# Projecting the keys and values of all heads ahead of their use and keeping them in DRAM, with the attention unrolled in steps of half a head

## What is computed

```python
x = x + jnp.tanh(g_xattn[0]) * _L0_xattn_ref(_layernorm(x), ids, ctx, ctx, ctx)
x = x + jnp.tanh(g_ffn[0]) * _L0_ffn_ref(_layernorm(x), w_gate, w_up, w_down)

# attention: b = 4 sequences, sq = skv = 256, H = 16 heads of HD = 128
q = (inputs_q @ Wq).reshape(b, sq, H, HD) * (1.0 / np.sqrt(HD))
k = (inputs_kv @ Wk).reshape(b, skv, H, HD)
v = (inputs_kv @ Wv).reshape(b, skv, H, HD)
scores = jnp.einsum('bqhd,bkhd->bhqk', q, k)
attn = jax.nn.softmax(scores, axis=-1)
ctx = jnp.einsum('bhqk,bkhd->bqhd', attn, v).reshape(b, sq, H * HD)
return ctx @ Wo
```

## Time and profile before

| | before |
|---|---|
| three executions | 628.35, 634.35, 634.07 us, median 634.07 |
| profiled execution | 627.44 us, of it the span 625.5 us |
| mean granted TensorE clock | 0.963 |
| PE busy | 548.1 us (88%) |
| DVE busy | 433.7 us (69%) |
| ACT busy | 312.3 us (50%) |
| POOL busy | 279.2 us (45%) |

### The profile page before, as it was taken

How to read it: one execution, slowest core, us unless ns; L and a number is a source line. 1 busy time by engine, 2 the same in 40 slices (tenths; PEclk the granted TensorE clock), 3 DMA queues, 4 the chain that set the end, 5 groups by cost and what they waited for, 6 DMA issues and landing times.

```text
span 625.5 us, 9791 instructions
## 1 busy us (share of the span) xinstructions
PE 548.1 (88%) x3396; PEld 475.5 (76%) x3402; DVE 433.7 (69%) x850; ACT 312.3 (50%) x602; POOL 279.2 (45%) x278
## 2 busy tenths in 40 slices
PE   1989668986789999999999999999955948999995
PEld 1777457765678999999999999999853747777773
DVE  6768899898745555655565655555579494888884
ACT  2620124653455555565555556555523723676772
POOL 2499055781044535356443444633326540544440
PEclk9999789998989999999999999999997979999999
DMA  8601000000001111010010100000002007777731
GB/s 267 228 1 34 0 2 1 1 1 1 2 1 33 35 26 43 27 43 17 10 42 25 42 25 25 1 26 9 2 28 74 1 0 245 237 232 234 248 125 67
DMA packets 26646, 38.51 MB, mean 62 GB/s; under 512 B 3696, under 2 KB 18160, under 8 KB 26608
## 3 DMA queue, kind: packets, MB, share of 16 engines
q1 hardware_dynamic: 26608, 38.01, 19.0%
HBM read 36.82 MB, written 1.18 MB: 61 GB/s over the span
## 4 chain that ended last, share of the span: by engine, by line
PE 66%; DVE 18%; issue 7%; ACT 5%; POOL 2%; DMA 1%; SPq 0%; DVEq 0%; POOLq 0%; ACTq 0%
PE ps L1158 20%; PE ps L1160 19%; PE ps L1159 19%; PE ps L1199 4%; DVE xr L867 2%; PE ps L1266 2%; DMA cT_raw<-in_ctx_t 1%; PE ps L1250 1%; DVE ln_y L787 1%; DVE st L771 1%; DVE h L792 1%; DVE ln_t L785 1%; DVE qtok L890 1%; ACT q2T L691 1%; DVE a_sel L853 1%
## 5 line engine op out<-in xcount | busy, mean ns | idle before, releaser
L511 POOL TENSOR_TENSOR probs<-probs,rsum 128x512 f32<-128x512 f32 x64 | 66.7, 1042 | 151.1 <-DVE rsum L937 147.3
L672 ACT ACTIVATE probs<-ps,nmax 128x256 f32<-128x256 f32 x128 | 59.3, 472 | 38.7 <-DVE nmax L932 38.7
L912 DVE TENSOR_TENSOR pT_lo<-ps,pT_hi 128x512 fp32r<-128x512 f32 x64 | 43.6, 683 | 13.1 <-ACT pT_hi L663 13.0
L754 ACT ACTIVATE e_hi<-e_r 128x1024 fp32r<-128x1024 f32 x32 | 33.9, 1061 | 34.4 <-PE ps L1160 24.6
L932 DVE TENSOR_REDUCE nmax<-ps 128x2 f32<-128x512 f32 x64 | 42.6, 686 | 9.8 <-PE ps L1160 9.8
L1126 DVE SCALAR_TENSOR_TENSOR e_r<-ps,cw_row 128x1024 f32<-128x1024 f32 x32 | 39.2, 1224 | 14.0 <-PE ps L1160 14.0
L458 POOL TENSOR_TENSOR w_hi<-w_raw,zeros 128x256 fp32r<-128x256 f32 x32 | 20.1, 628 | 59.4 <-PE ps L1160 38.1
L663 ACT ACTIVATE pT_hi<-ps 128x512 fp32r<-128x512 f32 x64 | 37.9, 598 | 14.7 <-PE ps L1199 14.7
L1199 PE MATMUL ps<-cst,probs 128*128 128x128 f32 x256 | 38.7, 277 | 2.3 <-POOL probs L511 2.3
L1158 PE MATMUL ps<-wv_hi,cT_lo 128*128 128x256 f32 x128 | 37.9, 296 | 3.0 <-DVE kT_lo L907 3.0
L1136 DVE TENSOR_TENSOR e_lo<-ps,e_hi 128x1024 fp32r<-128x1024 f32 x32 | 38.9, 1215 | 1.9 <-ACT ps L755 1.9
(11 more groups left out here) (246 smaller groups left out, 1872.9 us busy)
## 6 DMA issues: line engine op xcount, KB each, us to landing
cw_row<-cw_scratch SPq DMA_DIRECT2D x32, 512.0 KB, 4.9
wqk_raw<-in_w_qk SPq DMA_DIRECT2D x16, 256.0 KB, 2.7
w_raw<-in_w_t SPq DMA_DIRECT2D x32, 128.0 KB, 4.6
wv_raw<-in_w_v SPq DMA_DIRECT2D x8, 256.0 KB, 3.2
wo_raw<-in_w_o SPq DMA_DIRECT2D x16, 128.0 KB, 2.0
xr<-in_x SPq DMA_DIRECT2D x2, 512.0 KB, 6.0
cT_raw<-in_ctx_t SPq DMA_DIRECT2D x1, 1024.0 KB, 7.6
wraw<-in_w_gate_t SPq DMA_DIRECT2D x1, 1024.0 KB, 7.9
```

Source lines behind the costliest of these rows:

```text
L511: nc.gpsimd.tensor_tensor(probs[:, b, :, :], probs[:, b, :, :], rsum[:, b, :].unsqueeze(2).to_broadcast([P, 2, S]), ALU.mult).then_inc(pro ...
L672: last = nc.scalar.activation(probs[:, b, t, :], ps[:, bank[u], t * S:(t + 1) * S], ACT.Exp, bias=nmax[:, b, t:t + 1], accum_out=esum[:, b ...
L754: nc.scalar.activation(e_hi[e % 2][:, :], e_r[e % 2][:, :], ACT.Square).then_inc(e_hi_done, 1)
L912: ins = V.tensor_tensor(pT_lo[:, half, :, :].rearrange("p c q -> p (c q)"), src, pT_hi[:, half, :, :].rearrange("p c q -> p (c q)").bitcas ...
```

## The change

Keys and values of all 16 heads are projected outside the attention's own steps. They are 64 "units" of six matmuls of 512 columns: a K unit is one head and half of the tokens, a V unit four heads and 128 tokens. `FILLS` says where TensorE makes them: 22 in the expert and BitNet stages (after expert tiles 1, 2 and 6, after gate tiles 0, 1 and 2, and so on) and 42 in the first 21 attention steps, one in the middle ("m") and one at the end ("e") of a step. ScalarE copies each from PSUM to `kv_out` (four buffers), SP stores it to `k_scratch` or `v_scratch` in DRAM, and loads `k_raw` and `v_raw` of a head two or three steps before its use; ScalarE then makes the high part of these, GpSimd the low part. VectorE no longer makes low parts of keys and values.

The weights come as 23 blocks of 128x1024 (512 KB), each for four heads and one of K, V, Q, O, through two buffers `blk_raw`; ScalarE makes the high part (`block_high`), GpSimd the low part (`block_low`). Key and value blocks are loaded twice where both halves need them. `STEP_OF_BLOCK` says in which of the attention's steps a block is loaded and split.

The attention is 32 unrolled steps. Step u has the scores of u (one head, tokens of half u // 16), the transposes of u - 1, the query of u + 2, the output of u - 1 and the `Wo` product of u - 2. The banks are fixed by kind instead of a ring. The first half of the tokens is added to `xr` at step 18, so two accumulating banks suffice. The Hadamard matrices come by a load of their own. `Y0_PAIR` and the pairs of the BitNet stage differ, since banks 0 and 1 hold units in between. The transposes Q of the first tokens stand in a pair of the expert layer.

```diff
-        STEP = ["S0", "S1", "Y0", "S2", "K0", "S3", "K1", "T0", "Y1", "T1", "V0", "T2",
-                "Q0", "Q1", "T3", "O0", "V1", "O1"]
...
+        Q_BANK, S_BANK, P_BANK, O_BANK, Y_BANK, N1_PAIR = [0, 1], [2, 3], [4, 5], 1, [6, 7], 6
+        Y0_PAIR = [6, 2, 4, 6, 2, 4, 6, 0]
...
+        STEP_OF_BLOCK = {0: 10, 1: 11, 2: 12, 3: 13, 4: 14, 5: 15, 6: 16, 7: 17, 9: 18, 11: 19, 13: 20, 15: 21, 17: 22}
...
+        FILLS = {"a11": 1, "y2": 1, "y6": 4, "g0": 2, "g1": 1, "f0": 6, "g2": 1, "f1": 2, "d5": 1, "n0": 1, "d6": 2}
+        FRONT_UNITS = sum(FILLS.values())
+        for k in range(FRONT_UNITS, NF):
+            FILLS["me"[(k - FRONT_UNITS) % 2] + str((k - FRONT_UNITS) // 2)] = 1
...
+            def store(key):
+
+                for k in fills(key):
+                    kind, quad, n, g, j = UNITS[k]
+                    sp.wait_ge(kv_taken, k + 1)
...
+                    sp.dma_start(dst, src).then_inc(kv_stored[k % 4], 16)
...
+            for u in range(NU):
+                store("m" + str(u))
+                if u + 3 < NU:
+                    load_head(u + 3, "K")
+                if u + 2 < NU:
+                    load_head(u + 2, "V")
+                store("e" + str(u))
+                if u in STEP_OF_BLOCK:
+                    load_block(STEP_OF_BLOCK[u])
...
+            for u in range(NU + 1):
+                for b in range(GB):
+                    if u:
+                        probs_high(u - 1, b)
+                    if u < NU:
+                        exponent(u, b)
+                    if b == 0:
+                        take("m" + str(u))
+                if u + 2 < NU:
+                    query_high(u + 2)
+                    key_high(u + 2)
+                if u:
+                    output_high(u - 1)
+                if u + 1 < NU:
+                    value_high(u + 1)
+                take("e" + str(u))
+                if u in STEP_OF_BLOCK:
+                    block_high(STEP_OF_BLOCK[u])
...
+            for u in range(NU + 2):
+                for b in range(GB):
+                    if u < NU:
+                        scores(u, b)
+                    if 1 <= u <= NU:
+                        probs_back(u - 1, b)
+                    if b == 0:
+                        fill_units("m" + str(u))
+                if u + 2 < NU:
+                    query(u + 2)
+                for b in range(GB):
+                    if 1 <= u <= NU:
+                        output(u - 1, b)
+                    if u >= 2:
+                        add_head(u - 2, b)
+                fill_units("e" + str(u))
```

More of the change, by code:

```diff
@@ new lines, in _ @@
+            store("a11")
+            load_block(2)
+            store("y2")
+            load_block(3)
+            store("y6")
+            load_block(4)
+            store("g0")
+            load_block(5)
+            store("g1")
+            store("f0")
+            for u in range(2):
+                load_head(u, "K")
+                load_head(u, "V")
+            load_block(6)
+            store("g2")
+            load_block(7)
+            store("f1")
+            store("d5")
+            store("n0")
@@ L713, in _ @@
[L713 to L720 removed]
+                if i == 2:
+                    take("f1")
+                if i == NT:
+                    take("d5")
+                    block_high(6)
+                    norm_hi(1, 0, pair_of["N", 0])
+                    take("n0")
+                    key_high(0)
+                    value_high(0)
+                    key_high(1)
+                    block_high(7)
@@ new lines, in scores @@
+            def scores(u, b):
+                pe.wait_ge(q_done, u + 1)
+                pe.wait_ge(k_done, u + 1)
+                if u:
+                    pe.wait_ge(exp_done, GB * (u - 1) + b + 1)
+                else:
+                    wait_freed(last_user[2])
+                for t in range(2):
+                    at = slice(b * S + t * P, b * S + (t + 1) * P)
+                    last = product(ps[:, S_BANK[b], t * S:(t + 1) * S], both(qT_hi[u % 2], qT_lo[u % 2], A, at),
+                                   both(k_hi[u % 2], k_lo[u % 2], A, slice(b * S, (b + 1) * S)))
+                last.then_inc(s_filled, 1)
@@ new lines, in output @@
+            def output(u, b):
+                pe.wait_ge(p_done, GB * u + b + 1)
+                pe.wait_ge(v_done, u + 1)
+                if fills("m" + str(u + 1)):
+                    pe.wait_ge(kv_taken, fills("m" + str(u + 1))[-1] + 1)
+                elif u:
+                    pe.wait_ge(o_done, u)
+                for k in range(2):
+                    at = slice((2 * b + k) * P, (2 * b + k + 1) * P)
+                    last = product(ps[:, O_BANK, b * S:(b + 1) * S], both(v_hi[u % 2], v_lo[u % 2], A, at),
+                                   both(pT_hi, pT_lo, A, b, k, A), k == 0, k == 1)
+                if b == GB - 1:
+                    last.then_inc(o_filled, 1)
@@ new lines, in add_head @@
+            def add_head(u, half):
+                head, quad = u % NH, u % NH // 4
+                if head == 0 and half == 0:
+                    if u == 0:
+                        pe.wait_ge(hT_done, 2 * NG)
+                    else:
+                        pe.wait_ge(y2_taken, GN)
+                    for b in range(2):
+                        mm(ps[:, Y_BANK[b], :], zeros[:, 0:P], zeros[:, :], start=True, stop=False, skip_group_check=True)
+                pe.wait_ge(blk_done, BLOCKS.index(("O", quad)) + 1)
+                pe.wait_ge(o_done, u + 1)
+                at = slice(u % 4 * D, (u % 4 + 1) * D)
+                for n in (2 * half, 2 * half + 1):
+                    last = product(ps[:, Y_BANK[half], n % 2 * D:(n % 2 + 1) * D],
+                                   both(oT_hi[u % 2], oT_lo[u % 2], A, slice(n * P, (n + 1) * P)), both(wo_hi[quad], wo_lo[quad], A, at),
+                                   False, head == NH - 1 and n % 2 == 1, check=False)
+                if head == NH - 1:
+                    last.then_inc(y2_filled, 1)
```

781 lines of the change are left out of this document (370 added, 411 removed).

## The result

The changed kernel takes 685.9 us (median of four, 680.9 to 688.9) against 633.0 us of the kernel before beside it, a ratio of 1.085 (95% interval 1.079 to 1.092). The forecast was 651, the range 628 to 677. The sign and the main mechanism were right, the sum was 35 us short.

A forecast was written before the change was run, and what follows sets the result against it. TensorE alone was taken to bound the attention, VectorE the stage before BitNet. Profiled 627.4, minus 24 gained without stalls, plus 44 for stalls, gave 647.5; half of the median's 6.6 excess made 651 us, range 628 to 677.

The forecast's parts named there:

- the clock left out of a stall's price: Attention: each stall priced at 3.4 us from waits alone, with no fall of TensorE's clock.
- the second layer norm counted on TensorE alone: Attention step 1: the second norm added only 0.9 us, for its transposes.
- the front's rows of VectorE taken over as they were: Before BitNet: VectorE takes expert tile 5 in adds starting at 72.58, the second last about 74.55.
- the late block: 13 attention steps: a weight block's load, issued only after the last unit's store, keeps ScalarE waiting.
- The stalls: 13 attention steps take 12.75 us instead of 9.35: 3.4 per stall, 44 us in all (36 to 52).
- L: ScalarE's wait from its unit copy until the 512 KB block lands: 4.8 us taken, 4.2 to 5.4.
- a second idle of 0.6 us: Stalled attention steps: TensorE idles another 0.6 us for the low part of the second half's probabilities.
- rival (a): Same attention stalls, but TensorE's clock falls in each: 1.5 us times 13, 20 us more, 671; chance 0.27.
- The attention without stalls: First scores at 173.5 to the end at 442.1, with full steps of 9.35 us.
- The front: Ahead of attention: 8 us late at the last BitNet tile, another 3.3 after, first scores at 173.5.
- Rival (c): Attention: the wait for the block is hidden and the change gains, 607 us; chance 0.17.
- The point from which it decides: Rival (c) decides at L = 3.25 us; below that the kernel is faster.

The follow-up runs named there:

- early loads: The changed kernel with SP issuing each weight block's load ahead of the step's stores and loads in the 13 steps: 631.0 us, ratio 1.000.
- the split put behind: The changed kernel with both parts of the block's split moved behind the next step's second exponents and normalisation, loads still late: 634.0 us, ratio 1.001.
- the third experiment: The changed kernel with GpSimd's low parts of weight blocks 2 and 3 moved behind the last expert tile: 678.5 us, ratio 1.076.
- copy first: The changed kernel with ScalarE's copy of the mid-step unit moved ahead of that step's exponents, loads still late: 676.9 us, ratio 1.076.

## Why the prediction fell short, step by step

The profiled span was forecast at 625.5 - 24 + 44 = 645.5 and came at 685.4, 39.9 more. Three terms carry it, a little over 13 us each. (The forecast had 3.3 us on top for the median, which came 1.3 under the profiled execution, so the median was 35 off and not 40.) The steps that failed are the clock left out of a stall's price, the second layer norm counted on TensorE alone, and the front's rows of VectorE taken over as they were. The mechanism of the loss, the late block, was right.

**The stalls: 57.2 instead of 44.** This is the attention's length in the changed kernel less that with early loads, first scores to last `Wo` matmul, 339.4 - 282.1. Right: the place, the cause, the count of 13, the length of the wait (ScalarE's idle is 3.9 to 4.7 us, 4.3 in the mean; L was 4.8 in a range of 4.2 to 5.4), and the steps between them. One stall was 4.4 us in the mean (57.2 / 13) instead of 3.4. Three parts of its price were off:
- L is 4.3, 0.5 shorter: from the load's issue to ScalarE's start on the block it is 3.5 to 4.3 us, 3.9 in the mean, nearer to the lone load (3.7) than to the second of two (4.8).
- The output waits for ScalarE's copy of the middle unit, since they share bank 1. The prediction followed the chain to the low part of the probabilities only, 0.85 us earlier. The two nearly cancel: the printed waits of the 13 have their median at 2.98 us, forecast 2.65.
- The clock. The forecast left it out and had a second idle of 0.6 us in each step instead; rival (a) put it in at 2.2 less 0.6. Step 14 against 12 and 16 shows 1.5, and step 14, at full clock, has one wait and no second idle. Steps 3 to 8 take 13.7 to 15.4 us, 4.3 to 6.0 over 9.37, and the lower level stands behind at least 11 of the 13 stalls. Rival (a) was the right mechanism and should have been the forecast. What was argued against it, that 2.65 us of idle is shorter than the 3.45 of the earlier trace rows and follows dense work, did not hold: dense work ahead did not protect it. The Trainium skill (TensorE: Matmul & The Clock Gate, HAM oscillation) describes this fall at each wait for a transfer; this trace agrees in part, with 0.88 in steps 12 and 16, and at 1.00 in step 14 shows a wait of the same kind without it.

**The attention without stalls: 282.1 instead of 268.6.** The kernel with early loads has the steps bare. Steps 3 to 17 are 9.37 (forecast 9.35), steps 21 to 29 6.58 (6.55), step 18 11.67 (11.35). Three edges are not: step 0 took 7.7 (5.6), step 1 15.2 (8.85), and from the start of step 31 to the end 13.6 (10.35). In step 1 VectorE runs the second layer norm, 8 us of small operations, ahead of the maxima of the scores. The prediction counted this norm by its transposes on TensorE (0.9 us) and forgot it on VectorE. That the edges at step 0 and at the end are longer was not taken apart. ScalarE and TensorE in the kernel with early loads:

```profile
200.27 0.47 ACT L759 ACTIVATE probs<-ps,nmax 128x256 f32<-128x256 f32 x1 [4.84 <-DVE nmax L984]
```

```profile
201.92 0.55 PE L1198 MATMUL ps<-pT_hi,v_lo 128*128 128x256 f32 x1 [3.46 <-ACT kv_out L651]
```

Of the 8 us, 2.2 are once more a small operation of VectorE beside GpSimd's low part of a block:

```profile
195.06 2.36 DVE L856 TENSOR_TENSOR ln_t<-ln_t,ln_v 128x4 f32<-128x4 f32 x1
195.02 2.39 POOL L504 TENSOR_TENSOR wq_lo<-blk_raw,wq_hi 128x1024 fp32r<-128x1024 f32 x1 [1.01 <-ACT wq_hi L643]
```

With the split put behind, all repetitions of this operation took 0.16 us, the norm 5.8 us, and step 1 took 12.4 us. In the changed kernel, whose block comes late, step 1 took 13.2, 2.0 less than here; so the 57.2 us above are what the early load gave net of this, and the stalls alone cost some 59.

So the gain of the denser attention over the kernel before was 303.8 - 282.1 = 21.7 us and not 35.

**The front: 24.8 us late instead of 11.3.** Followed in order, the forecast was right as to which waits stand where, and late by what it had not counted. The transposes of the first tokens came at 77.75 (forecast 74.55), tile 7 at 84.19 (80.7), the first product at 90.63 (86.7): 3.9 us. The two operations that GpSimd's low parts held up account for it: with them out of the way the third experiment has it at 85.2, ahead of the forecast. The step that failed is the sentence that VectorE takes tile 5 in the adds that start at 72.58: it took the rows of before for VectorE as they were, while GpSimd had been idle at that place before and was given 4.7 us of work there. A rule was at hand. The Trainium skill (SBUF — State Buffer, Who interferes with whom) has VectorE and GpSimd share a pair of ports that one instruction holds to its end. The trace agrees in four rows: each of the slow operations ends within 0.1 us of GpSimd's.

The eighth product was forecast 8 us late and came 18.0 late, 6.1 beyond the 3.9. One part is the same lock in the third tile (2.3 us, then a wait of 2.5 us and half clock behind it): 3.0 us, by the kernel in which it did not fall on VectorE's operation. The units' work on TensorE is not the reason: the third tile took 12.2 us with two of them, and 9.3 us with six where the lock was absent. How the other 3 us divide is not settled. From there to the scores it was 6.8 us and not 3.3; this was not taken apart.

**Rival (c)**, the wait hidden, was 607 with the front as forecast. The two kernels that hide it took 631 and 634. The point from which it decides was right in kind, the gain that stands against it was not 24 us but about 0: 21.7 in the attention less the time lost ahead of it.

## What to carry to other kernels

Where one engine copies a tile out and then waits for a load, look in the issuing queue for the store of that same tile ahead of the load: the round trip is then paid in full, each time, and everything behind the wait pays with it. Moving the load ahead of the step's stores was worth 55 us of 686 here; putting the instruction that waits behind those that the critical engine needs next was worth 52. Price a regular stall at the lower clock too, and when an engine gets new work in a place where it was idle, ask which neighbour's small instructions run there.

## What the runs showed of the hardware

- Waits of TensorE between stretches of dense matmuls were followed by the lower clock level (256 columns in 0.21 us, up to about 264.0 in the stall shown above) behind a printed 2.03 us in one place (copy first) and not behind 2.52 us in another (changed kernel): the length of the wait alone did not decide it.
- VectorE's operations on 128x4 took 2.40, 2.38, 2.33 and 2.36 us beside GpSimd's 128x1024 subtraction (2.3 to 2.4 us), 0.16 to 0.23 us without it.
- 23 loads of 512 KB, most behind a 256 KB store, landed a median 3.9 us after their issue, a lone one before 3.7. With the doubled DMA traffic (75.8 MB instead of 38.5) and early loads, steps 3 to 17 stayed at 9.36 to 9.38 us.
